# Relative bias as a product of its own, crossed last products and a new step order in a two-layer decoder kernel

## What is computed

```python
# L0_attn: Nystroem attention, 16 heads of 8, 64 landmarks (means of two tokens)
kernel1, kernel2, kernel3 = softmax(Q Kl), softmax(Ql Kl), softmax(Ql K)
V = kernel2.T / max_column_sum
for _ in range(6):
    KV = kernel2 @ V
    V = 0.25 * V @ (13*I - KV @ (15*I - KV @ (7*I - KV)))
out = (kernel1 @ V @ (kernel3 @ v)) @ w_proj

# L0_xattn: 16 heads of 8 against ctx, with a relative bias
logits = q @ k.T * 8**-0.5 + (i - j) * w_rel[h]
out = softmax(logits) @ v @ w_proj

# L0_ffn: 8 experts, the best one per token
# L1_attn: causal attention, 16 heads of 8
# L1_xattn: 16 heads of 64 against ctx, with layer norms and a mask
# L1_ffn: 128 -> 512 -> 128, its weights mixed from 32 low-rank primitives
```

## Time and profile before

| | us |
|---|---|
| median of 3 runs | 2554.89 (2550.74 to 2559.74) |
| the profiled execution | 2548.0 |
| its span, first to last instruction | 2546.2 |
| PE busy | 2268.8 (89%), 40576 products |
| DVE busy | 1962.0 (77%) |
| ACT busy | 1450.1 (57%) |
| POOL busy | 373.3 (15%) |

### The profile page before, as it was taken

How to read it: one execution, slowest core, us unless ns; L and a number is a source line. 1 busy time by engine, 2 the same in 40 slices (tenths; PEclk the granted TensorE clock), 3 DMA queues, 4 the chain that set the end, 5 groups by cost and what they waited for, 6 DMA issues and landing times.

```text
span 2546.2 us, 95561 instructions
## 1 busy us (share of the span) xinstructions
PE 2268.8 (89%) x40576; PEld 1851.9 (73%) x40576; DVE 1962.0 (77%) x6185; ACT 1450.1 (57%) x5093; POOL 373.3 (15%) x516
## 2 busy tenths in 40 slices
PE   6589999999999999999999999999999999999875
PEld 4467777777777777777777777777777777777763
DVE  3258888878888887788888878888888788888753
ACT  0346565656656565565656566656565665656531
POOL 0001111111111111111111111111111111111111
PEclk9589999999999999999999999999999999999986
DMA  6000000000000000000000000000000000000000
GB/s 271 2 6 8 9 9 8 9 5 8 8 9 9 8 9 5 8 8 9 9 9 9 8 4 8 9 9 9 8 9 5 8 8 9 9 8 8 3 6 3
DMA packets 29529, 35.73 MB, mean 14 GB/s; under 512 B 3240, under 2 KB 27824, under 8 KB 28464
## 3 DMA queue, kind: packets, MB, share of 16 engines
q1 hardware_dynamic: 29104, 29.62, 3.4%
HBM read 27.51 MB, written 2.10 MB: 12 GB/s over the span
## 4 chain that ended last, share of the span: by engine, by line
PE 50%; DVE 28%; ACT 15%; issue 4%; POOL 0%; POOLq 0%; DVEq 0%; ACTq 0%
PE ps L525 28%; PE ps L528 8%; ACT probs L1079 5%; PE ps L785 3%; DVE probsT L1322 3%; PE ps L869 3%; ACT probs L1064 3%; PE ps L917 2%; ACT ey L1004 2%; DVE x_rows L1186 2%; DVE small L1227 2%; PE ps L802 2%; DVE qk_v L1310 1%; DVE probs L1454 1%; DVE p L1229 1%
## 5 line engine op out<-in xcount | busy, mean ns | idle before, releaser
L1112 POOL TENSOR_TENSOR small<-small,weights 128x1 f32<-128x1 f32 x256 | 149.6, 584 | 1188.9 <-DVE small L1175 1188.9
L1027 ACT ACTIVATE probs<-ps,small 128x128 f32<-128x128 f32 x1024 | 286.1, 384 | 30.6 <-DVE small L1315 29.0
L1322 DVE COPY probsT<-ps 128x512 f32<-128x512 f32 x384 | 262.9, 685 | 34.9 <-PE ps L528 31.3
L528 PE MATMUL ps<-weights,probs 128*128 128x128 f32 x1536 | 256.1, 291 | 33.9 <-ACT probs L1027 16.2
L1315 DVE TENSOR_REDUCE small<-ps 128x4 f32<-128x512 f32 x384 | 254.0, 683 | 16.4 <-PE ps L869 8.8
L528 PEld LDWEIGHTS ps<-weights,probs 128*128 128x128 f32 x1536 | 179.5, 146 | 86.3 <-ACT probs L1027 44.7
L1123 POOL TENSOR_TENSOR probs<-probs,small 128x256 f32<-128x256 f32 x128 | 108.9, 851 | 875.9 <-DVE small L1451 875.9
L948 ACT COPY x_T<-ps 128x128 f32<-128x128 f32 x128 | 34.1, 267 | 300.9 <-PE ps L528 300.9
L1079 ACT ACTIVATE probs<-ps,small 128x128 f32<-128x128 f32 x512 | 181.6, 375 | 18.6 <-DVE small L1315 17.1
L525 PE MATMUL ps<-wz,ss 64*64 64x72 f32 x6144 | 158.2, 230 | 35.8 <-DVE wz L1269 35.6
L525 PEld LDWEIGHTS ps<-wz,ss 64*64 64x64 f32 x6144 | 131.1, 138 | 67.7 <-DVE wz L1269 49.1
(11 more groups left out here) (200 smaller groups left out, 5385.4 us busy)
## 6 DMA issues: line engine op xcount, KB each, us to landing
weights<-in_wpack SPq DMA_DIRECT2D x1, 5703.5 KB
fc_B<-in_b SPq DMA_DIRECT2D x2, 2048.0 KB, 13.4
fc_A<-in_a SPq DMA_DIRECT2D x2, 2048.0 KB, 23.1
x_in_rows<-in_x SPq DMA_DIRECT2D x32, 64.0 KB, 1.8
x_in_T<-in_xT SPq DMA_DIRECT2D x32, 64.0 KB, 1.8
ctx_T<-in_ctxT SPq DMA_DIRECT2D x32, 64.0 KB, 1.9
ctx_rows<-in_ctx SPq DMA_DIRECT2D x32, 64.0 KB, 1.9
mask_i<-in_mask SPq DMA_DIRECT2D x32, 64.0 KB, 2.0
```

Source lines behind the costliest of these rows:

```text
L528: return nc.tensor.transpose(dst, src, ident)
L1027: ins = nc.scalar.activation(probs(s, g)[:, j], bank(s, SCORE_BANK[g], 128 * j, 128), ACT.Exp, bias=sm(s, "nb", 4 * g + j, 1), scale=-1.0)
L1112: nc.gpsimd.tensor_tensor(sm(s, out), sm(s, ve), w("mhalf"), ALU.pow).then_inc(sem(done, s), 1)
L1322: V.tensor_copy(probsT(s, n % 4).rearrange("p a b -> p (a b)"), bank(s, 2)).then_inc(sem("pT", s), 1)
```

## The change

The bias of the first cross attention leaves q and k. Two constants in bfloat16 hold it, made in the preamble: `rel_q` (rows 0 to 2 of each 32 are ones, rows 3 to 5 the position i) and `rel_k` (rows 0 to 2 are j times w_rel, rows 3 to 5 minus w_rel, each value cut in three bfloat16 pieces so that their sum is nearly the fp32 value). Each score bank begins with the product of these, over 32 rows and 512 columns, and the fp32 score product is added to it. With that, q and k have the form of the causal attention: weights `x_q` and `x_k` of 128 columns, q copied by ACT (`r1.q` moves from DVE to ACT), k laid out with `hmask` by one DVE operation. The first products of the iteration become one step with one wait, in which four tiles take turns; the last W step and n.w are crossed as the others, for which DVE reads their results in two and four pieces. All numbers of `PLACES` are new.

```diff
-PERIOD = 74.45336
+PERIOD = 74.79388
...
-        "rm.y1 138.034  rm.h3 138.035  rm.y2 140.456  rm.y3 140.569  r.ln2 143.788  r2.proj 146.641  "
...
+        "rm.y1 138.234  rm.h3 138.303  rm.y2 141.047  rm.y3 141.048  r.ln2 146.494  r2.proj 151.827  "
...
-                for g in range(TG):
-                    link(nc.vector.tensor_tensor(kaug[:, g], w("kpat"), w("kpos"), ALU.mult))
-                    link(nc.vector.tensor_scalar(kaug[:, g], kaug[:, g], w("x_rel", g, 1), None, ALU.mult))
+                nc.vector.tensor_copy(rel_q[:], w("ramp_q"))
+                link(nc.vector.tensor_tensor(left[:], every(w("ramp_k"), TJ), over(w("x_rel"), 128), ALU.mult))
+                for n in range(3):
+                    link(nc.vector.tensor_copy(part[:], left[:]))
+                    if n < 2:
+                        link(nc.vector.tensor_tensor(left[:], left[:], part[:], ALU.subtract))
+                    if n == 0:
+                        link(nc.vector.tensor_scalar(rel_k[:], part[:], w("piece", 0, 1), None, ALU.mult))
+                    else:
+                        link(nc.vector.scalar_tensor_tensor(rel_k[:], part[:], w("piece", n, 1), rel_k[:], ALU.mult, ALU.add))
...
-            for c in range(2):
-                pe.wait_ge(sem("n_eT", s), at("n_eT", s, 3 + c))
-                for i in range(4):
+            pe.wait_ge(sem("n_eT", s), at("n_eT", s, 4))
+            for i in range(4):
+                for c in range(2):
                     for m in halves:
                         t = k2T[M * c:M * c + M, i, m]
                         mm = one(PS[s][m, 1 - c, M * i:M * i + M], t, t)
-                mm.then_inc(sem("n_first_ps", s), 1)
-                yield f"n.kk{c}"
+            mm.then_inc(sem("n_first_ps", s), 1)
+            yield "n.kk"
...
-                            mm = one(PS[s][halves[m if last else m ^ g], g, PW * i + a:PW * i + PW], ss[halves[m], p, 0:M],
+                            mm = one(PS[s][halves[m ^ g], g, PW * i + a:PW * i + PW], ss[halves[m], p, 0:M],
...
-            for h in range(H):
-                _, _, p, m = heads(h)
-                mm = one(PS[s][m, 0, 16 * p:16 * p + HD], p2[m, p], ey[m, p, M:PW])
+            for i in range(4):
+                for g in range(2):
+                    p = 4 * g + i
+                    for m in range(2):
+                        mm = one(PS[s][halves[m ^ g], g, 16 * i:16 * i + HD], p2[halves[m], p], ey[halves[m], p, M:PW])
...
-                for g in range(WCOL[name][1] // 128):
-                    mm = one(bank(s, b, 128 * g, 128), w(name, 128 * g, 128), t)
-                mm.then_inc(sem("proj", s), 1)
+                one(bank(s, b, 0, 128), w(name), t).then_inc(sem("proj", s), 1)
...
+                    else:
+                        mmul(t, rel_q[quarters[g]], rel_k[quarters[g]], start=True, stop=False, skip_group_check=True)
+                for t, g in zip(to, groups):
+                    mmul(t, qc(s)[quarters[g]], k4(s)[quarters[g]], start=False, stop=True, skip_group_check=True
+                         ).then_inc(sem("s_ps", s), 1)
...
+            act.wait_ge(sem("proj", s), at("proj", s, 3 * (n_att - 1) + 1))
+            copy(qc(s), bank(s, 0, 0, 128)).then_inc(sem("a_q", s), 1)
+            yield f"{a}.q"
...
-                        ins = V.scalar_tensor_tensor(Y, src[:, :, M:PW], 0.25, uy[:, ps], ALU.mult, ALU.add)
+                        for to, at_ps in ((slice(0, 128),) * 2,) if g == 0 else zip(halves, halves[::-1]):
+                            ins = V.scalar_tensor_tensor(Y[to], src[at_ps, :, M:PW], 0.25, uy[to, ps], ALU.mult, ALU.add)
...
-            for m, half in enumerate(halves):
-                ins = V.tensor_tensor(w9[half, :, m, 0:HD], v[half], sm(s, "rd")[half].unsqueeze(2).to_broadcast([M, PAIRS, HD]),
-                                      ALU.mult)
+            for g in range(2):
+                v = bank(s, g, 0, 64).rearrange("p (a b) -> p a b", b=16)[:, :, 0:HD]
+                for m, half in enumerate(halves):
+                    ins = V.tensor_tensor(w9[half, 4 * g:4 * g + 4, m, 0:HD], v[halves[m ^ g]],
+                                          sm(s, "rd", 4 * g, 4)[half].unsqueeze(2).to_broadcast([M, 4, HD]), ALU.mult)
...
-                V.tensor_tensor(q4(s), bank(s, 0).rearrange("p (g t) -> p g t", g=TG), every(w("qaug"), TG),
-                                ALU.add).then_inc(sem("a_q", s), 1)
...
-                V.tensor_tensor(k4(s), bank(s, 1).rearrange("p (g t) -> p g t", g=TG), kaug[:], ALU.add).then_inc(sem("a_k4", s), 1)
...
+            V.tensor_tensor(k4(s), every(bank(s, 1, 0, 128), TJ), over(w("hmask"), 128), ALU.mult
+                            ).then_inc(sem("a_k4", s), 1)
```

82 lines of the change are left out of this document (29 added, 53 removed), and 86 rows, old and new, of the table PLACES.

## The result

The changed kernel takes 2569.3 us (median of 10 runs, 2555.4 to 2582.8); the kernel before took 2553.8 beside it (2550.7 to 2575.0). The ratio is 1.0059, 95% interval 1.0033 to 1.0085: slower by 0.6%, where 2.4% faster was forecast. The profiled execution has a span of 2567.2 us, against the earlier trace rows.

A forecast was written before the change was run, and what follows sets the result against it. TensorE was taken as the main bound, busy 66.96 of 72.62 us a batch, beside the batch's own chain; stretches summed to -2.0 us a batch, 31 x 2.0 = 62 us, giving 2493 us (-2.4%), range 2460 to 2542.

The forecast's parts named there:

- The terms of TensorE: Per batch: projections -1.41, bias product +0.60, kk -0.44, W5 -0.37, n.w -0.37; sum -1.99 us.
- The rule weighed: Different row tiles cannot access one PSUM bank simultaneously, so crossing W5 and n.w would gain nothing; forecast followed the profile row instead.
- A: Stretch of a batch from n.ln to n.a0, 4.34 us, called chain (VectorE's landmarks); forecast +0.2 us.
- B: Stretch from n.a0 to n.S0, 24.14 us, called TensorE's with VectorE nearly as full; forecast -1.1 us.
- C: Stretch from n.S0 to n.w, the iteration, 36.44 us with 3.18 us of waits, 0.3 of them to be filled; forecast -0.7 us.
- W2 is then about 0.9 later, but the same work is done when it runs: Third iteration: r1.y1 now ahead of n.W2 delays it about 0.9 us, without net loss since h0/h1 fill the gap behind.
- D: Stretch from n.w back to n.ln, 7.85 us, called TensorE's; forecast -0.4 us from n.w.
- so W5's 0.37 mostly goes: End of the iteration: n.w waits for VectorE's added small operations, +0.19 and about +0.3 us, taking most of W5's saving.
- rival 1: The chain keeps the gain, TensorE's savings going into waits: -0.8 us a batch, 2530 us; chance 0.20.
- The clock drops I leave as they are: Falls to 1.2 GHz taken as unchanged, worth 28 x 1.2 = 33 us, which may vanish or double.
- the third rival: No change: rival 1 with the new score product at its upper bound, or doubled clock drops; 2545 to 2562 us; chance 0.07.
- The fourth rival: Slower: third iteration's W2 and S3 delayed, chain 3.1 us longer against 2.0 saved, +1.1 a batch, 2589 us; chance 0.06.

The follow-up runs named there:

- new_code_old_order: The changed kernel's code with the table of places of the kernel before, kk and r1.q placed anew; 2569.5 us, ratio 1.0040-1.0088.
- before_fill: The kernel before with filler products in its own waits: two ahead of n.a0, three ahead of r1.z, one ahead of rf.h; 2554.8 us.
- kk_two: The changed kernel with the first products kk in two steps again; 2552.9 us, ratio 0.9986-1.0014.
- fill_three: The changed kernel with filler products ahead of kk (three), ahead of S0 (three) and r1.s23's bias products issued four times; 2551.9 us.
- two_fill_sharp: Changed kernel, kk in two steps, third iteration in old order, fills in waits but none ahead of S0, r1.s23's bias products four times; 2544.3 us.

## Why the prediction was wrong, point by point

- **The terms of TensorE.** Projections 2.08 to 0.7 as forecast. The bias product: r1.s23 takes 1191.51 to 1192.69 = 1.18 us against 1.09, +0.1 for a pair where 0.30 was taken; the two products on different rows start 4 ns apart in the trace and the score products 0.22 us behind them, while two over 128 rows start 0.22 us apart. kk, W5, n.w 0.63, 0.58, 0.58 where 0.66 was taken. The sum is -1.37 + 0.18 - 0.47 - 0.45 - 0.45 = -2.6 us, and so says the busy time (66.96 in the earlier trace rows, 64.36 in the batch shown): there was more to save than forecast.
- **The rule weighed.** The row was right against the Trainium skill's "TensorEngine Tiling (Array Packing)", Restrictions and Gotchas: crossed within their banks, W5 and n.w got faster by 0.45 us each. In the trace four of their products start within 0.02 us, two row halves into each bank, where before two did.
- **The stretches.** A +0.2 and B -1.1 hit. C, -0.7, measured +0.3: the step that failed is "of the 3.18 us of waits I let 0.3 be filled". Idle time grew by 1.1 us instead: in the means of the undisturbed batches W0 waits 0.66 us where it waited 0.41, n.w 0.55 where it did not wait, and the third iteration has waits of 0.48, 0.70, 0.23 and 0.64 us for 0.45, 0.85 and 0.21. "W2 is then about 0.9 later, but the same work is done when it runs" is not the step: from S2 to W2 it took 1.5 us more, and taking 1.1 of that back was worth 0.0 to 0.2 us. W5's share of C and D's -0.4 went into waits for VectorE's pieces (0.55 and 0.28 us). The text had seen it, "so W5's 0.37 mostly goes", and then summed the 0.37 in C all the same. Undisturbed batch -0.48 against -2.0: 1.5 x 31 = 47 us of the miss (43 by the batches without pauses, -0.62).
- **Whose time is it.** "B and D are TensorE's" rested on busy shares. new_code_old_order shows that in one fixed order TensorE's savings reach the end at 0.0 to 0.1 of 2.6 us. What I called rival 1, *the chain keeps the gain* (-0.8 a batch), is the mechanism, and it should have led: the waits it names rose, in C to 4.29 us. Its price was near what the batch shown gave, -0.7, but by luck: B gave 1.1 instead of 0.6, C lost 0.3 instead of nothing, and D gave 0.1 instead of 0.4.
- **The clock and the pauses.** "The clock drops I leave as they are": this step failed too. Time at 1.2 GHz rose from 3.17 to 4.51 us per batch, and what the disturbed batches cost doubled, from 1.04 to 2.08 us, 1.04 x 31 = 32 us. About half of that is not the clock: the 15 pauses take 0.64 us per batch, some 0.5 of it in disturbed batches. The prediction has no term for them, and the kernel before showed none. Twelve pauses stand in the stretch kk to W0, where the changed kernel also waits, and a fall follows each. I had named a doubling of the drops as possible and put it at 0.07, in the third rival; it came together with the first rival, and I had priced no world with both. The experiments show that filler in the waits prevents the falls behind the pauses and filler elsewhere does not. The Trainium skill, "TensorE: Matmul & The Clock Gate", Part 1, says that a monitor watches how busy the array is and gates its clock; the fills agree.
- **The fourth rival**, the third iteration, had the sign right by another cause: S2 to W2 did grow by 1.5 us, and taking it back gave 0.04 us per undisturbed batch (0.2 without pauses).
- **The ends.** The last stretch is as long as before (211.2 us); the first n.q copy came at 54.9 instead of 53.6, 1.3 us. The 15 kernels with the new preamble have it at 53.5 to 55.5, 54.9 in the mean, the five with the old one at 53.1 to 53.7, 53.4 in the mean: the new preamble costs 1.5 us, where about 0 was forecast for both ends.

Sum: 47 + 32 + 1 = 80 us in the profile, against 2567.2 - 2484 = 83 of its span (the other 3 lie in the first three batches, 219.2 against 214.9 us from the first n.q to the fourth) and 2569.3 - 2493 = 76 in the medians.

**What stays open.** What makes TensorE pause. That it waits for instructions fits every pause, but no run changed only the amount or the place of its instructions, and why the kernel before is spared while the fills of before_fill bring 13 pauses is not shown. Open is also why a pause is followed by a fall in some batches of a filled kernel and not in others, why a fall of 3.4 us at 31 to 33 us costs 1.4 to 1.9 us beyond the pauses of its batch and one at 65 costs 1.0, and why falls at 64 to 71 us come in every kernel (ahead of those of before TensorE has no long wait). That the fills in the new order take falls away is shown, by the sets with and without them and by the control; that waits alone bring falls is not, since kk_two has 14 with as much idle time as before, and 19 of the 153 early falls have no pause over 0.5 us ahead.

## What to carry to other kernels

Where an engine is 90% busy and waits often for short times, its work is not yet the bound: a saving counts only up to the next operation whose data another engine makes, so walk a term forward to that wait before it is summed. A saving on TensorE is also a new idle time, and with short waits in a row the clock may fall and take more than was saved; look at the batches with full clock and at those without apart, and among both at those in which the engine stands still though nothing that the profile shows holds it. If the clock falls behind such waits, try a few products without use inside the waits, each smaller than its wait: here they made a kernel that had lost 0.6% faster than before by 1.2%.

## What was not expected of the hardware

More work made the kernel faster: 1.9 us more products per batch, 17 us less in all (fill_three). One bf16 product of 128 x 512, 0.2 us, ahead of S0 decided over 22 us (two_fill_sharp), and did so by what it did to the clock, since the batches without pause or fall took the same time. In the kernel before, 3.17 us at 1.2 GHz cost 1.04 us per batch, a third of their length and not the half that a busy TensorE would lose. TensorE stands still for 0.5 to 1.9 us between two products, in every kernel but two, and goes on 1.1 to 3.0 us behind a 16 KB transfer of instructions. Two bf16 products on different 32 rows run at once: they start 4 ns apart and take 0.39 us for both.
